# Attention probabilities turned by a transposing DMA instead of by TensorE

## The chip, the cores and the metric

The kernel runs on one core of one Trainium2 chip. The metric is the device time of one execution in microseconds (us). In the names of the profile PE is TensorE, PEld its weight loads, DVE is VectorE, ACT is ScalarE, POOL is GpSimd, SP is the engine whose queue issues most DMAs (SPq is that queue). `m_...` is an SBUF tensor, `bank` a PSUM bank.

## The reference

A residual stream x of 16 sequences of 64 tokens with 512 features (1024 tokens) passes eight blocks: four cross-attentions to a context of the same size, each followed by a feed-forward block. The change touches three of the attentions, which in the names are a0, a2 and a3. Each has 32 heads of size 128 and full fp32 accuracy is wanted. Layer 0 in short (a2 adds a position bias per head and a mask; a3 has 4 key/value heads and takes as keys the context and x itself, 128 for each sequence):

```
x = x + attention(layernorm(x), ctx)
q = rms(x @ Wq.T);  k = rms(ctx @ Wk.T);  v = ctx @ Wv.T     # 32 query heads, 8 key/value heads in a0
p = softmax(q @ k.T / sqrt(128))                             # per head: tokens x keys
out = (p @ v) @ Wo.T                                         # sums over 32 heads x 128
```

The product p @ v sums over keys. TensorE sums over partitions, so p, which is made with tokens on partitions, has to be turned: keys to partitions, tokens to columns.

## The kernel before

The blocks follow one another in time: set-up, a0 (about 55 to 656 us), its feed-forward f0, the cross-attention x1, f1 (to about 900), a2 (900 to 1670), f2, a3 (1855 to 2316), f3. All five engines run in parallel; only semaphores tie them.

Every fp32 product is done as three fp16 matmuls (`mm3`, L84, L85, L86): each operand is split into a high part (the value rounded to fp16) and a low part (the rest), and hi*hi, hi*lo and lo*hi are summed in PSUM. So whatever feeds a product is evicted twice, by ACT as the high part and by DVE as the low one (source minus high part).

An attention is 64 units: 8 groups of 4 heads, times 8 tiles of 128 tokens. The order of all work is one list of events, `events` (L125 to L194), from which each engine takes its own part and keeps its order. A slot of this list works on several units at once, in this order: scores of unit b; a projection tile (or several); the reciprocal of the row sums, `rinv`, of b; squares of a weight that has been loaded (`w_squares`); **turn** of b-1; **mix** of b-2, which is p @ v; **out** of b-3, which multiplies by Wo and adds to x; the split of the loaded weight (`w_convert`). Eight slots are a period; slots 0 to 3 and 4 to 7 serve the two halves of a group. `periods` writes period 0, a loop over the middle ones, and the last ones.

The steps of one unit and their lines:

- scores: PE into bank 2 or 3; DVE scales, adds mask or bias and takes the maximum (a0: L835, L852; a3: L823); ACT takes the exponential into `m_E` (L427, in a3 L423); DVE the reciprocal (L866); POOL multiplies `m_E` by it (L893), after which `m_E` holds probabilities in fp32, [128 tokens x 4 heads of 64 or 128 keys];
- turn: PE transposes `m_E` into bank 4 by fp32 matmuls with an identity, of 128 columns each (L611: two in a0, four in a2 and a3); ACT writes the high part from bank 4 to `m_PT` (L435) and DVE the low part (L870);
- mix: PE multiplies `m_PT` with the values into bank 5, ACT (L440) and DVE (L875) split that into `m_A`;
- out: PE multiplies `m_A` with `m_wo_t`, DVE adds the result to x (L881).

Weights come by DMAs that SP issues (`load`, L261), into the two halves of `m_raw`: 1 MB each, in a0 256 KB for k and v. SP first waits until the half is free (`w_lo`). ACT then squares the slab (L309), PE sums the squares over partitions (L481), and in a later slot ACT and DVE split it (L314, L680). In a2 SP also issues one 128 KB bias tile per unit (L285), for which it waits until the bias two units back has been used (`biased`). SP carries nothing else inside the attentions, so it stands at its next wait and issues each load as soon as the buffer is free. Loads stand in even slots of SP's program (a0 and a2: slots 0, 2, 4, 6; a3: slots 0, 2); squares stand in slots 0, 1, 4, 5 in a0, and in even slots elsewhere.

Semaphores count finished steps: `probs` is POOL's multiply, `turned` PE's transposes, `turned_hi` and `turned_lo` the two evictions, `mixed` PE's p @ v.

Of the kernel before, what the change touches and what calls it, by code (L numbers as in the profile page):

```python
# [7 lines left out]
FP16 = mybir.dt.float16  # L8
# [3 lines left out]
ALU = mybir.AluOpType  # L12
ACT = mybir.ActivationFunctionType
# [79 lines left out]
class Attention:  # L93
# [6 lines left out]
    def __init__(self, k, layer, dram, before, before_count):  # L100
# [10 lines left out]
        self.NP, self.NK = len(self.pre), len(self.kinds)  # L111
        names = ["raw0", "raw1", "w_ss", "w_tot", "w_scale", "w_fac", "w_hi", "w_lo", "misc", "misc_read",
                 "proj", "proj_hi", "proj_lo", "scores", "biased", "top", "exped", "rinv", "probs",
                 "turned", "turned_hi", "turned_lo", "mixed", "mixed_hi", "mixed_lo", "outp", "xadd",
                 "stat", "rstd", "xn", "xt", "xt_hi", "xt_lo", "dve", "pool"]
        names += {0: ["k_tot", "k_rs", "k_n", "k_nhi", "k_nlo", "q_tot", "q_rs"],
# [10 lines left out]
        totals |= dict.fromkeys(("scores", "top", "exped", "rinv", "probs", "turned", "turned_hi", "turned_lo",  # L127
                                 "mixed", "mixed_hi", "mixed_lo", "outp", "xadd"), UNITS)
        totals |= {"biased": 0 if layer == 3 else UNITS}
# [142 lines left out]
    def sp(self, sp):  # L272
# [13 lines left out]

        def emit(t, events):
            kinds = {7: 1, 8: 0}.get(t, self.NK) if isinstance(t, int) else self.NK
            for slot in range(8):
                if self.layer == 2 and (not isinstance(t, int) or 0 <= 8 * t + slot - 4 < UNITS):  # L290
                    bias(t, slot - 4)
                if slot % 2 == 0 and slot // 2 < kinds:
                    n, kind = slot // 2, self.kinds[slot // 2]
                    g = at(t, 1, 0 if kind == "o" else 1)
                    self.load(sp, kind, g, self.NP + self.NK * 0 + n + (self.NK * parity(t)),
                         at(t, self.NK, self.NP + n - 1))
                if isinstance(t, int) and t == 8 and slot == 1:
                    self.next.load_tail(sp)
# [47 lines left out]
    def act(self, act):  # L346
# [7 lines left out]
        def emit(t, events):  # L354
            for e in events:
# [59 lines left out]
                elif e[0] == "scores":  # L415
                    b = e[1]
                    act.wait_ge(*s["top"].by(at(t, 8, b + 1)))
                    act.wait_ge(*s["turned"].by(at(t, 8, b - 1)))
# [12 lines left out]
                elif e[0] == "turn":  # L431
                    b = e[1]
                    act.wait_ge(*s["turned"].by(at(t, 8, b + 1)))
                    act.wait_ge(*s["mixed"].by(at(t, 8, b - 1)))
                    act.activation(self.pt_dst(b, 0), bank[4][:, 0:self.keys * HG], ACT.Copy).then_inc(s["turned_hi"].sem, 1)  # L435
# [26 lines left out]
    def pt_dst(self, b, part):  # L462
        return self.k.PT[:, b % 2, part, 0:self.keys * HG]
# [31 lines left out]
    def pe(self, pe):  # L495
# [22 lines left out]
        def emit(t, events):  # L518
            par = parity(t)
            for e in events:  # L520
# [85 lines left out]
                elif e[0] == "turn":  # L606
                    b = e[1]
                    pe.wait_ge(*s["turned_lo"].by(at(t, 8, b)))
# [4 lines left out]
                elif e[0] == "mix":  # L613
# [3 lines left out]
                    pe.wait_ge(*s["turned_lo"].by(at(t, 8, b + 1)))  # L617
# [3 lines left out]
                    pt_ = k.PT[:, b % 2]  # L621
                    if self.layer == 0:
                        for b2 in range(2):
                            lhs = [k.V[:, i, hf, b2, pt * P:(pt + 1) * P] for i in range(2)]
                            ins = mm3(pe, out[:, b2 * HG * S:(b2 + 1) * HG * S], lhs, [pt_[:, i, 0:HG * S] for i in range(2)])
                    elif self.layer == 2:
                        for h in range(4):
                            cols = slice(h * P, (h + 1) * P)
                            ins = mm3(pe, out[:, cols], [k.V[:, i, hf, pt, cols] for i in range(2)],
                                      [pt_[:, i, cols] for i in range(2)])  # L630
                    else:
                        for b2 in range(2):
                            cols = slice(b2 * 256, (b2 + 1) * 256)
                            ins = mm3(pe, out[:, cols], [self.values3(t, b, i, b2) for i in range(2)],
                                      [pt_[:, i, cols] for i in range(2)])
# [101 lines left out]
    def dve(self, dve):  # L737
# [16 lines left out]
        def emit(t, events):  # L754
            par = parity(t)
            for e in events:
# [110 lines left out]
                elif e[0] == "turn":  # L867
                    b = e[1]
                    dve.wait_ge(*s["turned_hi"].by(at(t, 8, b + 1)))
                    dve.tensor_tensor(self.pt_dst(b, 1), bank[4][:, 0:self.keys * HG], self.pt_dst(b, 0),  # L870
                                      ALU.subtract).then_inc(s["turned_lo"].sem, 1)
# [716 lines left out]
class AdapterFFN(TailFFN):  # L1588
# [3 lines left out]
    def __init__(self, k, layer, att, dram):  # L1592
# [3 lines left out]
        super().__init__(k, f"f{layer}", ["iota", "hw", "ht", "ht_s", "out"], att, dram, n, regions)  # L1596
# [177 lines left out]
    def base(self, pe, t):  # L1774
# [4 lines left out]
        if t == 2:  # L1779
            pe.wait_ge(*a["turned_lo"].by(UNITS))  # L1780
# [236 lines left out]
class Kernel:  # L2017


    def __init__(self, nc, ctx):  # L2020
# [34 lines left out]
        self.PT, self.A = sb("PT", [P, 2, 2, 512], FP16), sb("A", [P, 2, 2, 512], FP16)  # L2055
        self.bias_in = sb("bias_in", [P, 2, 256])
# [226 lines left out]
```

## Time and profile before

| what | us |
|---|---|
| median of 3 runs | 2360.66 (2359.34 to 2363.18) |
| profiled execution, its own time | 2360.68 |
| span of that execution in the trace | 2358.9 |
| PE busy, share of the span | 2179.8 (92%) |
| DVE busy | 1335.0 (57%) |
| ACT busy | 1138.0 (48%) |
| POOL busy | 541.1 (23%) |
| PE's share of the chain that ended last | 65% |
| share of DVE, ACT, and of "issue" in that chain | 14%, 11%, 7% |

The chain is followed back from the last instruction of the program, each time to what released it. "issue" is time in which an engine waited for nothing that the profile shows. A busy share is a mean over stages with different limits; the stages have to be looked at one by one. The mean clock that TensorE was granted is 0.974 of full speed. The share of the DMA engines in use is around a tenth in most of the attentions.

### The profile page before, as it was taken

To read this page: it belongs to the slowest core of one execution; us is meant where nothing else is said; L and a number is where in the kernel's file an instruction comes from. 1 tells how busy PE (TensorE), PEld (TensorE's weight loads), DVE (VectorE), ACT (ScalarE), POOL (GpSimd) and SP (SyncE) were. 2 spreads that over 40 slices of the span, in tenths; PEclk is the share of its full clock that TensorE was granted. 3 is DMA by queue.
4 is the path that set the end of the run, shared out by engine and by line. 5 is a ranking of instruction groups with operands and counts; after the bars stand their busy time and mean duration, and the time that the engine had idled before them with its cause. 6 is when DMAs were issued, how large, how long until landed. Compare 5 with 4: busy or idle time off the path is not lost.

```text
span 2358.9 us, 40756 instructions
## 1 busy us (share of the span) xinstructions
PE 2179.8 (92%) x14284; PEld 1224.4 (52%) x14284; DVE 1335.0 (57%) x2695; ACT 1138.0 (48%) x2988; POOL 541.1 (23%) x936
## 2 busy tenths in 40 slices
PE   4889898988999889999999999998879899999998
PEld 2555555555554434555555555555434455555564
DVE  5566666666653455556565655655642455555554
ACT  4566565656412235545455554543322466556551
POOL 3332323233220222221222222112310122222221
PEclk8999999999979999999999999999979999999999
DMA  3110101100021011111112111101210101011000
GB/s 121 46 46 24 47 24 47 42 28 19 25 107 47 37 56 66 66 48 56 58 46 65 49 66 48 48 12 41 90 36 1 37 37 36 36 37 48 5 33 36
DMA packets 27365, 106.91 MB, mean 45 GB/s; under 512 B 4074, under 2 KB 12522, under 8 KB 17186
## 3 DMA queue, kind: packets, MB, share of 16 engines
q1 hardware_dynamic: 26722, 104.36, 12.8%
q8 instruction: 112, 1.84, 0.3%
q14 instruction: 83, 0.68, 0.1%
q10 hardware_dynamic: 448, 0.03, 0.0%
HBM read 102.29 MB, written 2.10 MB: 44 GB/s over the span
## 4 chain that ended last, share of the span: by engine, by line
PE 65%; DVE 14%; ACT 11%; issue 7%; POOL 1%; DMA 0%; ACTq 0%; DVEq 0%; POOLq 0%
PE bank L84 18%; PE bank L85 17%; PE bank L86 17%; PE bank L1786 3%; ACT m_E L427 2%; PE bank L1432 2%; PE bank L611 2%; DVE m_Sm L835 2%; DVE m_x L881 2%; ACT m_arena L309 2%; ACT m_arena L409 1%; DVE m_A L875 1%; PE bank L1332 1%; DVE m_arena L680 1%; DVE m_nmax L852 1%
## 5 line engine op out<-in xcount | busy, mean ns | idle before, releaser
L781 DVE TENSOR_TENSOR m_arena<-bank,m_arena 128x512 f16<-128x512 f32 x320 | 221.0, 691 | 506.7 <-ACT m_arena L409 504.9
L84 PE MATMUL bank<-m_input_parts,m_arena 128*128 128x512 f16 x1088 | 415.9, 382 | 8.4 <-DVE m_arena L781 2.3
L85 PE MATMUL bank<-m_input_parts,m_arena 128*128 128x512 f16 x1088 | 415.9, 382 | 0.0
L86 PE MATMUL bank<-m_input_parts,m_arena 128*128 128x512 f16 x1088 | 415.6, 382 | 0.0
L427 ACT ACTIVATE m_E<-m_Sm,m_nmax 128x64 f32<-128x64 f32 (+1 forms) x512 | 185.4, 363 | 421.1 <-DVE m_nmax L852 236.7
L893 POOL TENSOR_TENSOR m_E<-m_E,m_rinv 128x512 f32<-128x512 f32 (+1 forms) x192 | 177.6, 925 | 862.1 <-DVE m_rinv L866 862.1
L409 ACT ACTIVATE m_arena<-bank 128x512 f16<-128x512 f32 x320 | 189.7, 593 | 231.8 <-PE bank L86 231.3
L84 PE MATMUL bank<-m_wo_t,m_A 128*128 128x512 f16 x768 | 293.2, 382 | 0.0
L85 PE MATMUL bank<-m_wo_t,m_A 128*128 128x512 f16 x768 | 292.8, 381 | 0.0
L86 PE MATMUL bank<-m_wo_t,m_A 128*128 128x512 f16 x768 | 292.4, 381 | 0.0
L423 ACT ACTIVATE m_E<-bank,m_nmax,m_qk 128x128 f32<-128x128 f32 x256 | 113.8, 454 | 182.3 <-DVE m_nmax L823 182.3
L84 PE MATMUL bank<-m_arena,m_input_parts 128*128 128x128 f16 (+1 forms) x768 | 188.8, 276 | 5.5 <-DVE m_arena L786 4.7
L86 PE MATMUL bank<-m_arena,m_input_parts 128*128 128x128 f16 (+1 forms) x768 | 188.8, 276 | 0.0
L85 PE MATMUL bank<-m_arena,m_input_parts 128*128 128x128 f16 (+1 forms) x768 | 188.8, 276 | 0.0
L890 POOL TENSOR_TENSOR m_w_scale<-m_w_tot,m_consts 128x1 f32<-128x1 f32 x82 | 44.8, 546 | 584.4 <-DVE m_w_tot L674 551.7
L86 PEld LDWEIGHTS bank<-m_input_parts,m_arena 128*128 128x128 f16 x1088 | 107.2, 99 | 130.5 <-issue 3.7
L881 DVE SCALAR_TENSOR_TENSOR m_x<-bank,m_osc,m_x 128x512 f32<-128x512 f32 x192 | 143.1, 745 | 52.8 <-PE bank L86 52.5
L84 PEld LDWEIGHTS bank<-m_input_parts,m_arena 128*128 128x128 f16 x1088 | 107.1, 98 | 118.8 <-issue 5.7
L85 PEld LDWEIGHTS bank<-m_input_parts,m_arena 128*128 128x128 f16 x1088 | 107.0, 98 | 105.0 <-issue 3.7
L870 DVE TENSOR_TENSOR m_PT<-bank,m_PT 128x512 f16<-128x512 f32 (+1 forms) x192 | 112.2, 584 | 69.7 <-ACT m_PT L435 68.5
L611 PE MATMUL bank<-m_ident,m_E 128*128 128x128 f32 x640 | 104.1, 278 | 49.3 <-POOL m_E L893 49.2
L875 DVE TENSOR_TENSOR m_A<-bank,m_A 128x512 f16<-128x512 f32 x192 | 131.2, 683 | 0.2
(278 smaller groups left out, 4337.3 us busy)
## 6 DMA issues: line engine op xcount, KB each, us to landing
m_raw<-a_q SPq DMA_DIRECT2D x24, 1024.0 KB, 4.8
m_raw<-a_o SPq DMA_DIRECT2D x24, 1024.0 KB, 4.8
m_raw<-a_k SPq DMA_DIRECT2D x9, 1024.0 KB, 5.0
m_raw<-a_v SPq DMA_DIRECT2D x9, 1024.0 KB, 4.9
m_bias_in<-bias SPq DMA_DIRECT2D x64, 128.0 KB, 2.0
m_arena<-f_w SPq DMA_DIRECT2D x3, 1024.0 KB, 7.5
m_x<-x SPq DMA_DIRECT2D x2, 1024.0 KB, 6.9
m_arena<-ctx_t SPq DMA_DIRECT2D x4, 512.0 KB, 12.3
```

What stands on the lines that cost most here:

```text
L84: pe.matmul(out, lhs[0], rhs[0], start=first, stop=False)
L85: pe.matmul(out, lhs[0], rhs[1], start=False, stop=False)
L86: return pe.matmul(out, lhs[1], rhs[0], start=False, stop=last)
L409: act.activation(self.dest(name, part, 0), self.shaped(name, src), ACT.Copy).then_inc(s["proj_hi"].sem, 1)
L423: ins = act.activation(k.E[:, b % 2, cols], bank[2 + b % 2][:, cols], ACT.Exp, bias=k.nmax2[:, b % 2, h:h + 1], scale=qk, accum_out=k.rsum ...
L427: ins = act.activation(k.E[:, b % 2, cols], k.Sm[:, b % 2, cols], ACT.Exp, bias=k.nmax[:, b % 2, h:h + 1], accum_out=k.rsum[:, b % 2, h:h ...
L611: ins = pe.transpose(bank[4][:, j * P:(j + 1) * P], k.E[:, b % 2, j * P:(j + 1) * P], k.ident[:, :])
L781: ins = dve.tensor_tensor(self.dest(name, part, 1), self.shaped(name, bank[m % 2][:, :]), self.dest(name, part, 0), ALU.subtract)
L870: dve.tensor_tensor(self.pt_dst(b, 1), bank[4][:, 0:self.keys * HG], self.pt_dst(b, 0), ALU.subtract).then_inc(s["turned_lo"].sem, 1)
L875: dve.tensor_tensor(self.mix_dst(b, 1), self.mix_src(), self.mix_dst(b, 0), ALU.subtract).then_inc(s["mixed_lo"].sem, 1)
L881: dve.scalar_tensor_tensor(out=k.x[:, pair, :], in0=bank[6][:, :], scalar=k.osc[:, g:g + 1], in1=k.x[:, pair, :], op0=ALU.mult, op1=ALU.ad ...
L893: pool.tensor_tensor(out, a, b, op).then_inc(sem.sem, 1)
```

## The change

In a0, a2 and a3 (`self.moved` is true for all three) PE no longer transposes. In the step **turn**, ACT copies `m_E` from SBUF, as the high part in fp16, into a new SBUF tensor `m_split`; DVE subtracts it from `m_E` and writes the low part beside it; SP then issues one transposing DMA, which turns both parts of a unit into `m_PT`: [128 x 512] fp16 or 128 KB in a0, [128 x 1024] or 256 KB in a2 and a3. Mix on PE waits for the landing (`pt0`, `pt1`, one semaphore for each half of `m_PT`), not for DVE. SP waits, ahead of each transposing DMA, for the low part of the unit (`split_lo`) and for the mix of the unit two back, which frees `m_PT`. ACT waits, ahead of each high part, for the transposing DMA two units back, which frees `m_split`. ACT's exponential of a unit, which in before waited for PE's transposes of two units back, now waits for DVE's low part of it. In a0 the loads are in slots 0, 1, 4, 5 of SP's program instead of 0, 2, 4, 6. The event list, and with it the place of turn on ACT and DVE, is unchanged. Lines after the edits are 4 to 36 higher in the changed kernel.

```diff
@@ sp() @@
+        def turn(t, b):
+            n = 2 * HG * self.keys
+            sp.wait_ge(*s["split_lo"].by(at(t, 8, b + 1)))
+            sp.nop(nofuse=True)
+            sp.wait_ge(*s["mixed"].by(at(t, 8, b - 1)))
+            sp.nop(nofuse=True)
+            sp.dma_start_transpose(k.PT[:, b % 2].rearrange("p i n -> p (i n)")[:, 0:n].rearrange("p (h n) -> p h n", n=P),
+                                   k.split[:, b % 2].rearrange("p i n -> p (i n)")[:, 0:n])\
+                .then_inc((s["pt0"], s["pt1"])[b % 2].sem, 16)
...
                 if self.layer == 2 and (not isinstance(t, int) or 0 <= 8 * t + slot - 4 < UNITS):
                     bias(t, slot - 4)
-                if slot % 2 == 0 and slot // 2 < kinds:
-                    n, kind = slot // 2, self.kinds[slot // 2]
+                n = {0: 0, 1: 1, 4: 2, 5: 3}.get(slot, 4) if self.layer == 0 else 4 if slot % 2 else slot // 2
+                if n < kinds:
+                    kind = self.kinds[n]
                     g = at(t, 1, 0 if kind == "o" else 1)
                     self.load(sp, kind, g, self.NP + self.NK * 0 + n + (self.NK * parity(t)),
                          at(t, self.NK, self.NP + n - 1))
+                if self.moved and (not isinstance(t, int) or 0 <= 8 * t + slot - 5 < UNITS):
+                    turn(t, slot - 5)
@@ ScalarE @@
-                    act.wait_ge(*s["turned"].by(at(t, 8, b - 1)))
+                    act.wait_ge(*s["split_lo" if self.moved else "turned"].by(at(t, 8, b - 1)))
...
+                    if self.moved:
+                        act.wait_ge(*s["probs"].by(at(t, 8, b + 1)))
+                        act.wait_ge(*self.pt_here(t, b - 2))
+                        act.activation(self.split_dst(b, 0), k.E[:, b % 2, 0:self.keys * HG], ACT.Copy)\
+                            .then_inc(s["split_hi"].sem, 1)
+                        continue
@@ TensorE @@
-                elif e[0] == "turn":
+                elif e[0] == "turn" and not self.moved:
...
-                    pe.wait_ge(*s["turned_lo"].by(at(t, 8, b + 1)))
+                    pe.wait_ge(*(self.pt_here(t, b) if self.moved else s["split_lo"].by(at(t, 8, b + 1))))
@@ VectorE @@
+                    if self.moved:
+                        dve.tensor_tensor(self.split_dst(b, 1), k.E[:, b % 2, 0:self.keys * HG], self.split_dst(b, 0),
+                                          ALU.subtract).then_inc(s["split_lo"].sem, 1)
+                        continue
```

**SP in a0.** This is the end of the loop body of the middle periods in SP's program before. `m_raw<-a_o` is the load of a 1 MB slab of Wo; `w_lo` says that the buffer half is free.

```order
L261 DMA m_raw<-a_o 128x2048 [waits w_lo]
L252 REGISTER_ALU
L261 ISA [waits w_lo]
L261 DMA m_raw<-a_k 128x512
L252 REGISTER_ALU
L261 ISA [waits w_lo]
L261 DMA m_raw<-a_q 128x2048
L252 REGISTER_ALU
L261 DMA m_raw<-a_v 128x512 [waits w_lo]
L212 REGISTER_ALU
L212 COMPARE_AND_BRANCH
```

Four loads of a period stand in a row, with nothing between them but SP's wait for a free buffer half.

The same place in the program after, from the load of `a_o` on for four slots, L297 being the transposing DMA:

```order
L265 DMA m_raw<-a_o 128x2048 [waits w_lo]
L293 REGISTER_ALU
L297 DMA_TRANSPOSE m_PT<-m_split 128x4x128 [waits split_lo,mixed]
L256 REGISTER_ALU
L265 ISA [waits w_lo]
L265 DMA m_raw<-a_k 128x512
L293 REGISTER_ALU
L297 DMA_TRANSPOSE m_PT<-m_split 128x4x128 [waits split_lo,mixed]
L293 REGISTER_ALU
L297 DMA_TRANSPOSE m_PT<-m_split 128x4x128 [waits split_lo,mixed]
L293 REGISTER_ALU
L297 DMA_TRANSPOSE m_PT<-m_split 128x4x128 [waits split_lo,mixed]
```

Between a load and the next now stand transposing DMAs, each with its wait for DVE's low part of a unit. A load cannot be issued before the transposing DMA ahead of it in the list has been.

**SP in a3.** The start of the loop body in SP's program before:

```order
L212 ISA
L261 ISA [waits w_lo]
L261 DMA m_raw<-a_o 128x2048
L252 REGISTER_ALU
L261 ISA [waits w_lo]
L261 DMA m_raw<-a_q 128x2048
L252 REGISTER_ALU
L261 DMA m_raw<-a_o 128x2048 [waits w_lo]
```

Here too the loads follow on one another. The start of the loop body after:

```order
L265 ISA [waits w_lo]
L265 DMA m_raw<-a_o 128x2048
L293 ISA
L295 REGISTER_ALU [waits split_lo]
L297 DMA_TRANSPOSE m_PT<-m_split 128x8x128 [waits mixed]
L293 REGISTER_ALU
L295 REGISTER_ALU [waits split_lo]
L297 DMA_TRANSPOSE m_PT<-m_split 128x8x128 [waits mixed]
L256 REGISTER_ALU
L265 ISA [waits w_lo]
L265 DMA m_raw<-a_q 128x2048
```

The load of `a_q`, that followed directly on that of `a_o`, now stands behind the transposing DMAs of two slots. In a2 each slot also has its bias DMA, which stands ahead of the load and the transposing DMA of the same slot.

**PE in a3.** The end of a projection tile, turn and the start of mix in PE's program before:

```order
L85 MATMUL bank<-m_input_parts,m_arena 128x512
L86 MATMUL bank<-m_input_parts,m_arena 128x512
L609 REGISTER_ALU [waits turned_lo]
L611 MATMUL bank<-m_ident,m_E 128x128 [waits probs]
L611 MATMUL bank<-m_ident,m_E 128x128 x3
L84 ISA [waits turned_lo,mixed_lo]
L84 MATMUL bank<-m_PT,m_arena 128x256
L85 MATMUL bank<-m_PT,m_arena 128x256
L86 ISA
L86 MATMUL bank<-m_PT,m_arena 128x256
```

Turn stands between the tile and mix. The same place after:

```order
L85 MATMUL bank<-m_input_parts,m_arena 128x512
L86 MATMUL bank<-m_input_parts,m_arena 128x512
L648 REGISTER_ALU [waits mixed_lo]
L84 ISA [waits pt0]
L84 MATMUL bank<-m_PT,m_arena 128x256
L85 MATMUL bank<-m_PT,m_arena 128x256
L86 ISA
L86 MATMUL bank<-m_PT,m_arena 128x256
```

The four transposes of L611 are gone with their wait for POOL; mix starts right behind the projection tile and waits for the landing.

## Rows read from the trace of the kernel before

**Rows 1.** Busy by stretch: a0, a2, a3, one period of a3; columns: stretch, length, engines.
```profile
80.00:560.00 480.00, 428.84 (x3963) 268.04 (x3961) 307.10 (x719) 285.29 (x888) 148.95 (x251) 0.98 0.11 37
...
900.00:1620.00 720.00, 717.28 (x4514) 384.00 (x4512) 422.71 (x768) 360.42 (x860) 147.85 (x262) 1.00 0.15 50
...
1855.00:2270.00 415.00, 407.26 (x2701) 237.17 (x2700) 238.89 (x436) 246.65 (x693) 86.79 (x149) 1.00 0.09 31
...
2045.90:2102.60 56.70, 56.02 (x372) 32.64 (x370) 33.08 (x61) 34.29 (x96) 12.26 (x22) 1.00 0.11 37
```

**Rows 2.** Waits of ACT and PE, 80 to 560 us; columns: total us, times, longest.
```profile
ACT m_E L427 <- DVE m_nmax L852: 194.5, 52, 5.5
...
PE bank L611 <- POOL m_E L893: 32.0, 13, 2.6
```

**Rows 3.** Waits of PE, 900 to 1620 us: its only one.
```profile
PE bank L84 <- DVE m_arena L781: 2.7, 2, 1.9
```

**Rows 4.** Chain that ended last, a2; columns: start us, us, what.
```profile
1287.74 0.44 PE bank L611 x4
```

**Rows 5.** Waits of DVE on PE and of PE, 1945 to 2190 us.
```profile
DVE m_x L881 <- PE bank L86: 2.3, 7, 0.4
...
PE bank L481 <- ACT m_arena L309: 3.5, 5, 0.8
```

**Rows 6.** Timeline: low part, then squares of the next slot's load; a0, a3.
```profile
330.48 0.42 DVE L870 TENSOR_TENSOR m_PT<-bank,m_PT 128x256 f16<-128x256 f32 x1
...
336.19 1.90 ACT L309 ACTIVATE m_wo_t<-m_raw 128x2048 bf16<-128x2048 f32 x1
...
2102.95 0.66 DVE L870 TENSOR_TENSOR m_PT<-bank,m_PT 128x512 f16<-128x512 f32 x1
...
2108.69 1.92 ACT L309 ACTIVATE m_wo_t<-m_raw 128x2048 bf16<-128x2048 f32 x1
```

**Rows 7.** Timeline: low part, then its mix; a0, a2, a3, last unit.
```profile
310.71 0.39 DVE L870 TENSOR_TENSOR m_PT<-bank,m_PT 128x256 f16<-128x256 f32 x1
...
313.71 0.28 PE L84 MATMUL bank<-m_PT,m_arena 128*128 128x256 f16 x1
...
1292.22 0.69 DVE L870 TENSOR_TENSOR m_PT<-bank,m_PT 128x512 f16<-128x512 f32 x1 [1.39 <-ACT m_PT L435]
...
1302.77 0.22 PE L84 MATMUL bank<-m_PT,m_arena 128*128 128x128 f16 x1
...
2085.27 0.66 DVE L870 TENSOR_TENSOR m_PT<-bank,m_PT 128x512 f16<-128x512 f32 x1
...
2087.30 0.27 PE L84 MATMUL bank<-m_PT,m_arena 128*128 128x256 f16 x1
...
2303.62 0.68 DVE L870 TENSOR_TENSOR m_PT<-bank,m_PT 128x512 f16<-128x512 f32 x1
...
2304.96 0.28 PE L84 MATMUL bank<-m_PT,m_arena 128*128 128x256 f16 x1 [0.29 <-DVE m_A L875]
```

**Rows 8.** Page, group of the transposes: count, busy us, mean ns, idle before.
```profile
L611 PE MATMUL bank<-m_ident,m_E 128*128 128x128 f32 x640 | 104.1, 278 | 49.3 <-POOL m_E L893 49.2
```

**Rows 9.** SP's time for the issue of a copy: ns min/median/max.
```profile
L261 SPq DMA_DIRECT2D m_raw<-a_o x24: 328/333/423, 43.1 to 2178.4; - x24
```

**Rows 10.** Page, DMA issues: KB each, median us to landing.
```profile
m_raw<-a_o SPq DMA_DIRECT2D x24, 1024.0 KB, 4.8
...
m_bias_in<-bias SPq DMA_DIRECT2D x64, 128.0 KB, 2.0
```

**Rows 11.** DVE's L680, two inputs in SBUF, by itself: ns min/median/max.
```profile
L680 DVE SCALAR_TENSOR_TENSOR m_wo_t<-m_raw,m_w_scale,m_wo_t x25: 2341/2344/2352, 60.5 to 2232.8; 128x2048 f16<-128x2048 f32 x25
```

**Rows 12.** Timeline: POOL's multiply beside a low part (330.48), and beside L680.
```profile
330.53 0.61 POOL L893 TENSOR_TENSOR m_E<-m_E,m_rinv 128x256 f32<-128x256 f32 x1 [2.78 <-DVE m_rinv L866]
...
1907.93 1.04 POOL L893 TENSOR_TENSOR m_E<-m_E,m_rinv 128x512 f32<-128x512 f32 x1
1908.34 2.78 DVE L680 SCALAR_TENSOR_TENSOR m_arena<-m_raw,m_w_scale,m_arena 128x2048 f16<-128x2048 f32 x1 [0.26 <-ACT m_arena L314]
```

More of the change, by code:

```diff
@@ L126, in __init__ @@
         totals |= dict.fromkeys(("xn", "xt", "xt_hi", "xt_lo"), TILES)
-        totals |= dict.fromkeys(("scores", "top", "exped", "rinv", "probs", "turned", "turned_hi", "turned_lo",
+        totals |= dict.fromkeys(("scores", "top", "exped", "rinv", "probs", "split_hi", "split_lo",
                                  "mixed", "mixed_hi", "mixed_lo", "outp", "xadd"), UNITS)
+        totals |= {"turned": 0 if self.moved else UNITS}
+        totals |= dict.fromkeys(("pt0", "pt1"), 16 * (UNITS // 2) if self.moved else 0)
         totals |= {"biased": 0 if layer == 3 else UNITS}
@@ L432, in emit @@
                     b = e[1]
+                    if self.moved:
[4 more added lines that the diff above has]
+                        continue
                     act.wait_ge(*s["turned"].by(at(t, 8, b + 1)))
                     act.wait_ge(*s["mixed"].by(at(t, 8, b - 1)))
-                    act.activation(self.pt_dst(b, 0), bank[4][:, 0:self.keys * HG], ACT.Copy).then_inc(s["turned_hi"].sem, 1)
+                    act.activation(self.pt_dst(b, 0), bank[4][:, 0:self.keys * HG], ACT.Copy).then_inc(s["split_hi"].sem, 1)
                 elif e[0] == "mix":
@@ L462, in pt_dst, with split_dst, pt_here @@
     def pt_dst(self, b, part):
-        return self.k.PT[:, b % 2, part, 0:self.keys * HG]
+        n = self.keys * HG
+        return self.k.PT[:, b % 2].rearrange("p i n -> p (i n)")[:, part * n:part * n + n]
+    def split_dst(self, b, part):
+        n = self.keys * HG
+        return self.k.split[:, b % 2].rearrange("p i n -> p (i n)")[:, part * n:part * n + n]
+    def pt_here(self, t, b):
+        return (self.s["pt0"], self.s["pt1"])[b % 2].by(at(t, 64, 16 * (b // 2 + 1)))
     def mix_src(self):
@@ L620, in emit @@
                     out = bank[5]
-                    pt_ = k.PT[:, b % 2]
+                    pt_ = [self.pt_dst(b, i) for i in range(2)]
                     if self.layer == 0:
@@ L624, in emit @@
                             lhs = [k.V[:, i, hf, b2, pt * P:(pt + 1) * P] for i in range(2)]
-                            ins = mm3(pe, out[:, b2 * HG * S:(b2 + 1) * HG * S], lhs, [pt_[:, i, 0:HG * S] for i in range(2)])
+                            ins = mm3(pe, out[:, b2 * HG * S:(b2 + 1) * HG * S], lhs, pt_)
                     elif self.layer == 2:
@@ L629, in emit @@
                             ins = mm3(pe, out[:, cols], [k.V[:, i, hf, pt, cols] for i in range(2)],
-                                      [pt_[:, i, cols] for i in range(2)])
+                                      [pt_[i][:, cols] for i in range(2)])
                     else:
@@ L634, in emit @@
                             ins = mm3(pe, out[:, cols], [self.values3(t, b, i, b2) for i in range(2)],
-                                      [pt_[:, i, cols] for i in range(2)])
+                                      [pt_[i][:, cols] for i in range(2)])
                     ins.then_inc(s["mixed"].sem, 1)
```

15 lines of the change are left out of this document (9 added, 6 removed).

## The prediction

> **What bounds the kernel now.** I read the busy time by stage first, then the waits of each engine in a stage, then the chain, then single slots in the timeline. The stage table shows that the three attentions differ [rows 1]. In a2 PE is busy 717.28 of 720 us, and its waits add up to 2.7 us [rows 3]: PE sets the end, and a transposition on PE costs its full time, 0.44 us for four [rows 4]. In a0 PE is busy 428.84 of 480 us, DVE 307.10, ACT 285.29 [rows 1], so none is full. There ACT's one wait is for DVE, 194.5 us, and PE waits 32.0 us for POOL [rows 2]: ACT and DVE hand one unit's work to and fro, and PE has room. In a3 PE is busy 56.02 of a period of 56.70 us [rows 1], but DVE waits only 2.3 us for PE in 245 us, 7 times [rows 5]: PE and the pair of ACT and DVE have nearly the same length.
>
> **The change, part by part.** Against the profiled run, 2360.68 us; the median is 2360.66, so no conversion is needed.
>
> *Transposes off PE.* 640 go, 104.1 us of busy time [rows 8]; in the chain four cost 0.44 us, since they overlap in the pipeline [rows 4], so all are worth 70 us where PE is the bound. In a2 all but the last seven slots are: 57 x 0.44 = -25 us. In a3 DVE's wait for PE, 2.3 us in 4.3 periods [rows 5], is what can be taken from the pair: 0.53 a period, -4 over 7, and -3 in the seven tail slots with 0.44 each, where PE is nearly alone: -7. In a0 the bounds are 0 and 64 x 0.22 = -14, and a further -32 if PE's wait for POOL's multiply counted [rows 2]. It does not set the pace, since ACT waits for DVE and not for PE; I take -2, near the end of 0.
>
> *Two splits from SBUF instead of PSUM.* The same number of instructions of the same size on ACT and DVE. The low parts take 0.42 us in a0 and 0.66 in a3 [rows 6]; a tenth more or less of these in the 64 slots of a0 and of a3 would be +-7 us. I take 0. POOL's multiply no longer has to end before a transpose in the same slot on PE, but before ACT's copy of the same unit one slot later: nothing waits.
>
> *192 transposing DMAs on SP.* Before has none, so two unknowns: D, from the end of DVE's low part to the landing, and h, the time for which SP cannot issue what is queued behind. With h goes q, by which the transposition's data delay a load behind it. For D the nearest rows are 2.0 us for a copy of 128 KB and 4.8 for 1 MB [rows 10], with 128 KB and 256 KB to turn; turning is extra work and a copy's landing is the least, so I take 2.4 in a0 and 3.0 in a2 and a3. For h+q the ends are 0.33 us, a copy's issue [rows 9], and 4.8, if SP stands until landing. I take 1.5, which is between the copy's issue and its landing of 2.0; it is my least certain number.
>
> *Who waits for D.* Mix of a unit starts long after its low part: 2.61 us in the tightest slot of a0, 9.86 in a2, 1.37 in a3 [rows 7] (start less start and duration of the low part). In a0 2.4 fits. In a2 D is hidden, unless it were over 9. In a3 mix is later by 3.0 - 1.37 = 1.6 us; PE needs 56.0 - 8 x 0.44 = 52.5 of 56.7 us in a period now and can run behind by that. At worst both places a period where DVE waits for PE pay 1.6 - 0.44 each, 14 x 1.2 = +16; at best nothing. I take +2. The last unit of each attention has no other work to hide it: low part to mix was 0.66 us [rows 7], and this becomes D: 2 x 2.34 + 1.74 = +6.
>
> *Loads behind the transposing DMA.* This is the step that decides. SP issues the load of a slot only after the transposing DMA of the slot before, and this only after DVE's low part. Behind SP's wait stand the load, in a2 the next bias too, and ACT's squares wait for the load; ACT is half of the pair that bounds a0. In a0 a squares instruction on a 1 MB slab begins 336.19 - 330.90 = 5.29 us after the low part of the slot before [rows 6], and the load needs h+q and 4.8 us [rows 10]. Over is h+q - 0.49 = 1.0 us; o and q in seven periods and one more o are 15 such loads: +15. The 256 KB loads are smaller and have the time. In a3 the same gap is 2108.69 - 2103.61 = 5.08, less 0.44 as PE hands over earlier: h+q + 4.8 - 4.64 = 1.66 us, for the eight loads of Wo, +13. The loads of q there have squares two slots after o's and I take them as hidden. In a2 the slot is 12 us long and holds PE only; a late load or bias first uses up the pair's slack of several us: 0. If that cover were gone, each us would cost up to 57.
>
> *Sum.* a0 -2 + 15 = +13; a2 -25; a3 -7 + 2 + 13 = +8; the last units +6. Together +3: 2363.5 us. Each us of h+q moves it by 23.
>
> **The rivals.**
>
> *A. The transposing DMA is as cheap as a copy.* h+q = 0.33 and D = 2.0, the copy's rows. Then the 15 loads of a0 are in time, a3's eight pay 0.49 each: a0 -2, a2 -25, a3 -7 + 4, the last units +4: -26, 2335 us. For it: DMA engines are idle nine tenths of the time (share 0.11 to 0.15) [rows 1]. [...]
> [...]
>
> *B. SP stands until the transposition has landed.* h+q = D = 3.0: a0 -2 + 15 x 2.51 = +36, a2 -25, a3 -7 + 2 + 8 x 3.16 = +20, last units +6: +37, 2398 us. With 4.8 for all three: a0 +63, a3 +33 + 16, last units +12: +99, 2460. It decides from h+q = 1.6 on. [...] Against: a copy of 1 MB needs only 333 ns there [rows 9].
> [...]
>
> *C. A lock between DVE and POOL.* The low part now has two inputs in SBUF, as L680 has. L680 takes 2.34 us by itself [rows 11] but 2.78 when POOL's multiply had begun 0.41 us before [rows 12]. DVE's reciprocal frees POOL's multiply and is followed by the low part: at 330.48 DVE was first by 0.05 us [rows 6, 12]. If POOL came first, DVE would wait up to 0.6 us in a0 and 1.0 in a3. The timeline has the two side by side, on the chain, in about 70 slots of a0 and a3 (330.48 is the first kind of it, 4 heads of 64): 70 x 0.7 = +50 on top, 2413 us. Against: DVE is the earlier one in almost all.
> [...]
>
> *D. All of PE's time comes back.* 70 us and part of the 49.3 us that PE waited [rows 8]: some 2280. Against: PE has no place on the handing over between ACT and DVE in a0.
>
> **How the numbers follow.** My forecast, with h+q from 0.8 to 2.5, has .38, A .24, B .26, C .08, D .04. The measurement can tell 0.2%, 4.7 us. The forecast lies within that, but its own range is 2345 to 2387, since 0.2 us of h+q already crosses it: of .38, .06 is faster, .16 the same, .16 slower. Faster: .06 + .24 + .04 = .34; same .16; slower .16 + .26 + .08 = .50. The range of 8 in 10 reaches from A's time to above C's and into B's: 2334 to 2430.
>
> **What would show it.** The profile after has rows for the transposing DMA on SP: its time there is h, issue to landing is D's part. My steps are right if a2's slots shrink by 0.44 us each, if ACT waits for `m_raw` ahead of L309 in a0 15 times by about 1 us and in a3 8 times by 1.7, and PE waits for `m_PT` ahead of mix only at the three ends. A is right if these waits on `m_raw` are missing; B if SP's row is as long as the landing and the waits are over 2.5 us; C if the low part's mean grows by half. I am wrong as a whole if a2 does not get faster, which would mean that the bias or the loads come late there, or if D is beyond 5 us, so that every mix of a0 and a3 waits.

## The result: 2438 us, slower by 3.3%

| | median us | runs | ratio to before, 95% interval |
|---|---|---|---|
| before | 2361.92 | 2359.34 to 2364.53 | |
| changed kernel | 2438.12 | 2433.88 to 2440.76 | 1.0328 [1.0312, 1.0343] |
| forecast | 2363.5 | range 2334 to 2430 | |

The profiled executions took 2360.68 and 2433.88 us (spans 2358.9 and 2432.0), so the traces account for 73.1 us of the 76.2 between the medians. I split this by the starts of the 192 mixes on PE. "Body" is from the first mix of an attention to that of unit 56, "end" from there to the last unit's.

| us against before | body | last eight units | sum |
|---|---|---|---|
| a0 | +15.8 | +19.4 | +35.2 |
| a2 | -20.0 | +23.1 | +3.1 |
| a3 | +20.0 | +20.5 | +40.5 |
| other blocks | | | -5.7 |

The stage table of the changed kernel; columns as in rows 1. It answers to the first two of them, to a3 and to one period of a3.

```profile
80.00:560.00 480.00, 413.55 (x3774) 251.87 (x3773) 297.56 (x693) 281.96 (x863) 145.96 (x245) 0.97 0.17 48
900.00:1620.00 720.00, 713.15 (x4348) 364.06 (x4347) 423.63 (x771) 367.25 (x862) 182.60 (x271) 1.00 0.28 72
1905.00:2320.00 415.00, 370.76 (x2364) 200.50 (x2362) 229.35 (x416) 237.88 (x655) 97.00 (x146) 1.00 0.28 68
2045.78:2105.60 59.82, 53.16 (x340) 28.80 (x339) 33.20 (x62) 34.54 (x95) 14.02 (x23) 1.00 0.28 70
```

a2 is as full of PE as before [rows 1], and its slots fell by 0.44 us each, 12.14 to 11.70. In a3 PE fell from 407 to 371 us busy in 415: over a period it is no longer the bound, and a period is 59.8 us where it was 56.7. From mix to mix, the plain slots of a3 fell by the same 0.44 us (6.94 to 6.50), but three slots of a period rose, in the median from 7.0 to 9.4, from 7.8 to 9.7 and from 7.2 to 8.3 us. The other five are plain.

SP's own time for the transposing DMA (ns, minimum, median, maximum), and its time to landing; then, from the page, the landing of the copies and transpositions. They answer to [rows 9, 10].

```profile
L297 SPq DMA_TRANSPOSE m_PT<-m_split x192: 1189/1232/2472, 86.6 to 2374.9; - x192
...
DMA to landing us min/median/max: 2.4/3.0/4.8
```
```profile
m_raw<-a_o SPq DMA_DIRECT2D x24, 1024.0 KB, 4.9
...
m_bias_in<-bias SPq DMA_DIRECT2D x64, 128.0 KB, 2.2
m_PT<-m_split SPq DMA_TRANSPOSE x192, 3.0
```

So h is 1.2 us and the landing 2.4 us for 128 KB and 3.0 for 256 KB. To the landing come 0.13 us from the low part's end to SP's start and 0.14 from the landing to PE's: low part to mix is at least 2.65 us in a0 and 3.3 in a3.

**The body.** ACT's waits in a0 (80 to 560 us) and in a3 (1900 to 2320 us) of the changed kernel; the last line is a3's; columns: total us, times, longest.

```profile
ACT m_arena L326 <- DMA m_raw<-a_q: 6.8, 6, 1.5
ACT m_wo_t L326 <- DMA m_raw<-a_o: 5.0, 6, 1.3
...
ACT m_wo_t L326 <- DMA m_raw<-a_o: 10.7, 7, 1.9
```

ACT waits for the loads ahead of its squares as forecast: 11.8 us in 12 loads of a0, 0.98 each where 1.0 was forecast, and 1.5 in a3 where it was 1.66. Neither wait was there before.

**The ends.** Here is most of the loss, 63.0 of 73.1 us, and the prediction had 6. SP's queue and the router's matmuls of the block that follows a0, in the kernel before:

```profile
623.25 0.34 SPq L1124 DMA_DIRECT2D m_arena<-f_gate  x1
...
623.64 0.43 SPq L1124 DMA_DIRECT2D m_arena<-f_b  x1
...
631.21 0.96 PE L1168 MATMUL bank<-m_arena 128*128 128x8 f32 x8
```

and in the changed one, where the line numbers are 35 higher:

```profile
650.84 0.61 POOL L928 TENSOR_TENSOR m_E<-m_E,m_rinv 128x256 f32<-128x256 f32 x1 [2.37 <-DVE m_rinv L897]
650.89 0.84 DVE L902 TENSOR_TENSOR m_split<-m_E,m_split 128x256 f16<-128x256 f32 x1
...
651.86 1.19 SPq L297 DMA_TRANSPOSE m_PT<-m_split  x1
653.16 0.52 SPq L1159 DMA_DIRECT2D m_arena<-f_gate  x1
653.73 0.42 SPq L1159 DMA_DIRECT2D m_arena<-f_b  x1
...
658.75 1.88 PE L1203 MATMUL bank<-m_arena 128*128 128x8 f32 x8 [9.82 <-DMA m_arena<-f_b]
```

The blocks that follow an attention load their weights through the same queue (`load_tail`, five or so DMAs). Before, SP had nothing ahead of them and issued `f_b` 7.6 us before PE's router matmuls. Now the transposition of unit 60 stands ahead, and with it the wait for that unit's low part; `f_b` is issued 5 us before the matmuls, and PE waits 9.8 us for it. The chain of the changed kernel goes through it:

```profile
653.16 0.52 SPq L1159
...
653.73 4.98 DMA m_arena<-f_b
...
658.75 1.88 PE bank L1203 x8
660.62 0.44 PE bank L84
661.07 0.43 PE bank L85
```

The matmuls behind the wait take 0.43 us where they took 0.22. The granted clock is 0.50 there, the lower of the two levels in this trace (1.00 and 0.50), and stays so until 663.9: PE works 5.15 us at that level, which leaves some 2.6 us behind. In a2 the same wait is 14.4 us (for `f_bt`), in a3 11.0 (for `f_bm`): 35.2 us in the three.

The other part of the ends is the landing. PE's waits from 640 to 690 us of the changed kernel:

```profile
PE bank L84 <- DMA m_PT<-m_split: 10.2, 4, 3.1
PE bank L1203 <- DMA m_arena<-f_b: 9.8, 1, 9.8
```

Not one unit waits for its transposition at the end of an attention, but three to five (13.3 us in 3 waits in a2, 11.3 in 5 in a3): in the last period there are no projection tiles, and each slot is a chain of exponential, split, transposition, mix.

The lower clock costs more in the ends than behind these three waits. The three ends of the changed kernel, columns as in rows 1:

```profile
627.30:688.20 60.90, 40.83 (x325) 26.46 (x323) 34.93 (x86) 20.07 (x82) 17.56 (x20) 0.83 0.15 38
1615.90:1697.50 81.60, 51.14 (x329) 32.49 (x328) 39.93 (x79) 21.18 (x67) 19.07 (x20) 0.77 0.23 54
2316.00:2378.10 62.10, 39.80 (x252) 25.27 (x250) 32.36 (x62) 21.79 (x67) 15.70 (x16) 0.84 0.26 60
```

Before, the granted clock was 1.00, 0.94 and 1.00 in them. PE's work at the lower level rose from 6.8 to 36.3 us. Half of such work is lost, an estimate from the matmuls' 0.43 against 0.22 us, so the clock is some 15 of the 63 us. PE's idle time in the ends rose from 16.3 to 72.9 us.

### The profile page after: what moved, and what is told of

Its sections match the earlier page's. It is cut to its first block, busy times and chain, and to the rows that moved or that the text cites. A ratio compares the mean times of both kernels' runs of the same rounds, so it can differ in the third digit from the quotient of the medians.

```text
span 2432.0 us, 40109 instructions
## 1 busy us (share of the span) xinstructions
PE 2133.5 (88%) x13644; PEld 1158.0 (48%) x13644; DVE 1343.1 (55%) x2695; ACT 1145.5 (47%) x2988; POOL 595.5 (24%) x936
## 2 busy tenths in 40 slices
DMA packets 197347, 148.82 MB, mean 61 GB/s; under 512 B 174059, under 2 KB 182507, under 8 KB 187171
## 3 DMA queue, kind: packets, MB, share of 16 engines
q1 hardware_dynamic: 196706, 146.33, 21.8%
## 4 chain that ended last, share of the span: by engine, by line
PE 51%; DVE 15%; ACT 14%; issue 11%; DMA 6%; POOL 1%; SPq 1%; ACTq 0%; DVEq 0%; POOLq 0%
PE bank L84 13%; PE bank L86 13%; PE bank L85 13%; ACT m_E L444 2%; PE bank L1821 2%; PE bank L1467 2%; DMA m_raw<-a_o 2%; ACT m_E L440 2%; DMA m_PT<-m_split 2%; ACT m_arena L426 2%; DVE m_x L916 2%; DVE m_split L902 1%; DVE m_Sm L866 1%; PE bank L1367 1%; DVE m_arena L711 1%
## 5 line engine op out<-in xcount | busy, mean ns | idle before, releaser
L928 POOL TENSOR_TENSOR m_E<-m_E,m_rinv 128x512 f32<-128x512 f32 (+1 forms) x192 | 206.4, 1075 | 700.5 <-DVE m_rinv L897 700.5
L84 PE MATMUL bank<-m_wo_t,m_A 128*128 128x512 f16 x768 | 299.3, 390 | 0.0
L85 PE MATMUL bank<-m_wo_t,m_A 128*128 128x512 f16 x768 | 298.4, 389 | 0.0
L86 PE MATMUL bank<-m_wo_t,m_A 128*128 128x512 f16 x768 | 297.3, 387 | 0.0
L84 PE MATMUL bank<-m_PT,m_arena 128*128 128x256 f16 (+1 forms) x512 | 118.9, 251 | 80.5 <-DMA m_PT<-m_split 78.1
L902 DVE TENSOR_TENSOR m_split<-m_E,m_split 128x512 f16<-128x512 f32 (+1 forms) x192 | 119.4, 622 | 97.4 <-ACT m_split L453 96.3
```

The costliest lines, as they stand in the source:

```text
L84: pe.matmul(out, lhs[0], rhs[0], start=first, stop=False)
L85: pe.matmul(out, lhs[0], rhs[1], start=False, stop=False)
L86: return pe.matmul(out, lhs[1], rhs[0], start=False, stop=last)
L902: dve.tensor_tensor(self.split_dst(b, 1), k.E[:, b % 2, 0:self.keys * HG], self.split_dst(b, 0), ALU.subtract).then_inc(s["split_lo"].sem, 1)
L928: pool.tensor_tensor(out, a, b, op).then_inc(sem.sem, 1)
```

## Experiments

All ratios are to the kernel before on the same chip. The table gives the same split as above, in us against before.

| run | median us | ratio, 95% interval | a0 body, end | a2 body, end | a3 body, end |
|---|---|---|---|---|---|
| changed kernel | 2438.12 | 1.0328 [1.0312, 1.0343] | +15.8 +19.4 | -20.0 +23.1 | +20.0 +20.5 |
| e1_tail | 2406.37 | 1.0190 [1.0173, 1.0207] | +16.0 +10.4 | -20.2 +9.1 | +21.3 +8.3 |
| e2_queue | 2400.25 | 1.0155 [1.0138, 1.0172] | +3.2 +11.6 | +0.2 +15.5 | +2.2 +12.1 |
| e3_loads | 2410.71 | 1.0200 [1.0179, 1.0221] | +1.9 +19.6 | -22.8 +22.4 | +8.6 +20.7 |
| e4_both | 2376.30 | 1.0064 [1.0047, 1.0081] | +2.0 +6.6 | -22.8 +8.2 | +8.7 +10.2 |
| e5_only2 | 2344.41 | 0.9927 [0.9911, 0.9944] | -0.2 0.0 | -22.5 +8.9 | 0.0 0.0 |
| e6_only0 | 2369.27 | 1.0037 [1.0023, 1.0051] | +3.8 +12.1 | +1.1 +1.5 | +2.3 0.0 |
| e7_only3 | 2383.77 | 1.0095 [1.0079, 1.0112] | +0.4 +0.2 | +0.8 +1.5 | +9.6 +9.9 |
| e9_half | 2373.96 | 1.0059 [1.0042, 1.0076] | +0.8 0.0 | +0.9 +1.5 | +4.4 +8.7 |
| e8_best | 2339.03 | 0.9907 [0.9891, 0.9924] | +0.3 0.0 | -21.8 +1.0 | +0.1 0.0 |
| e10_squares | 2384.34 | 1.0098 [1.0076, 1.0120] | 0.0 0.0 | +0.9 +1.5 | +7.7 +11.4 |
| e11_before_sq | 2362.43 | 1.0007 [0.9997, 1.0018] | +0.2 0.0 | +0.2 0.0 | +1.0 0.0 |
| e12_two | 2347.65 | 0.9942 [0.9920, 0.9963] | +2.0 0.0 | -20.7 +0.8 | +7.1 -0.5 |

Bodies of attentions in which a run left the transposes on PE repeat to 2.3 us in this split, which is then its error. The time between the attentions moves by up to 5.8 us. The split belongs to the one profiled execution of a run, and this is not always near the median: that of e4_both is 7.8 us under it, that of e6_only0 5.0 above.

### e1_tail: the next block's loads earlier in the queue

```diff
+                if isinstance(t, int) and t == 8 and slot == 0:
+                    self.next.load_tail(sp)
                 if self.moved and (not isinstance(t, int) or 0 <= 8 * t + slot - 5 < UNITS):
                     turn(t, slot - 5)
-                if isinstance(t, int) and t == 8 and slot == 1:
-                    self.next.load_tail(sp)
```

> The changed kernel, with one edit: SP issues the loads of the feed-forward block that follows an attention ahead of the transposing DMA of unit 59 instead of behind that of unit 60. Theory T (the loads of the next block stand behind the transposing DMAs in SP's queue): PE's waits ahead of the router's matmuls (L1203), 9.8, 14.4 and 11.0 us in the changed kernel, go, and with them some 2 us each for matmuls at half clock behind them: 2438 - 41 = 2397 us, at most 2405. Theory H (the time is lost in the bodies of the attentions, by SP's 1.2 us for each transposition and by the landing): less than 3 us change, 2435 to 2438.

2406.37 us, 32 less. The bodies did not move. In the timeline of this run SP issues `f_b` ahead of unit 59's transposition, and PE's router matmuls have no wait:

```profile
639.15 1.19 SPq L297 DMA_TRANSPOSE m_PT<-m_split  x1
...
641.02 0.42 SPq L1159 DMA_DIRECT2D m_arena<-f_b  x1
...
645.59 7.48 SPq L297 DMA_TRANSPOSE m_PT<-m_split  x2
...
651.06 1.29 PE L1203 MATMUL bank<-m_arena 128*128 128x8 f32 x6
```

Theory T holds in its mechanism; it had expected 41 us, and the time came out 1 us above its limit of 2405. The profiled executions are 30.2 us apart. In them the three ends gave back 35.2 us, which is what the three waits were. The clock gave back less than the 2 us for each wait: PE's work at the lower level in the ends fell only from 36.3 to 29.4 us, as PE goes on waiting for its transpositions there (35.8 us, 34.8 in the changed kernel). The other 5 us are longer times in a3's body, between a2 and a3, and behind a3; no run shows why.

### e2_queue: the order of the queue without a transposition

```diff
@@ the kernel before, sp(); and loads in the slots of the changed kernel @@
+                if not isinstance(t, int) or 0 <= 8 * t + slot - 5 < UNITS:
+                    b = slot - 5
+                    sp.wait_ge(*s["turned_lo"].by(at(t, 8, b + 1)))
+                    sp.nop(nofuse=True)
+                    sp.wait_ge(*s["mixed"].by(at(t, 8, b - 1)))
+                    sp.nop(nofuse=True)
```

> The kernel before, with PE's transposes, in which SP only gets the waits of the changed kernel at the same places (DVE's low part of a unit, the mix two units back) and its slots of loads; no transposing DMA. It tells the order of the queue from the transposition's own time. Theory T: the next block's loads come behind the low part of unit 60, f_b lands at about 641 against a need at 631 in a0, the same in a2 and a3: three waits of about 10 us and 2 us each of half clock, 2362 + 36 = 2398 us; in the bodies the loads are just in time (5.2 against 5.3 us), 0 to 5 us more. Theory H: without a transposition there is nothing to lose, 2362 to 2366.

2400.25 us: 38 us slower than before with not one transposition moved. The kernel's PE waits from 600 to 660 us, from 2310 to 2345 and from 1630 to 1690 us show the three waits of theory T, 34 us together:

```profile
PE bank L1175 <- DMA m_arena<-f_b: 10.3, 1, 10.3
...
PE bank L1175 <- DMA m_arena<-f_bm: 11.1, 1, 11.1
...
PE bank L1175 <- DMA m_arena<-f_bt: 12.8, 1, 12.8
```

So half of a loss of 76 us comes from the order of one queue, without the price of a single transposition; most of it lies in the ends (39.2 us of the profiled execution's 43.9), as in the changed kernel.

### e3_loads and e4_both: weight loads one slot earlier

```diff
@@ in place of the choice of n for each slot @@
+                due = [(t, n) for n in range(1, kinds)
+                       if slot == ({1: 0, 2: 3, 3: 4}[n] if self.layer == 0 else 2 * n - 1)]
+                if t == 0 and slot == 0:
+                    due.insert(0, (t, 0))
+                if slot == 7 and t not in (7, 8):
+                    due.append((t + 1 if isinstance(t, int) else (t[0], t[1] + 1), 0))
+                for u, n in due:
```

> The changed kernel, in which each weight load stands one slot earlier in SP's queue, ahead of the transposing DMA that it followed; the loads of the next block stay where they are. Theory of the prediction (ACT's squares wait for the load): ACT's waits for m_raw, 11.8 us in 12 loads of a0 and 6.5 in 4 of a3, go: 15 x 1.0 + 8 x 1.6 = 28 us less, 2410. Rival L (the landing of the transposition takes the place of the load at once, as PE waits for m_PT in a3 already): a0 gains 15, a3 under 4, 2420. Rival: squares were not on the path, under 5 us change.

2410.71 us, 27 less: the expected number. ACT has no wait for `m_raw` left in a0 or a3. The bodies fell by 13.9 us in a0 and by 11.4 in a3, against 15 and 13 in the prediction. Rival L is wrong for a3: PE's other waits did not take the place of this one.

e4_both has this edit and that of e1_tail.

> Both edits of the two runs before it in the changed kernel: next block's loads early and weight loads one slot early. If they add up: 2438 - 41 - 28 = 2369 us; by rival L 2379. What then is left against the kernel before (2362) is the landing of the transpositions in a3's slots and in the last units, less the 25 us that a2 gains.

2376.30 us, 62 less than the changed kernel against 59 of the two single runs (32 and 27): they add up. It is 7 above the 2369 expected, which is what e1_tail had lacked already. What is left over the kernel before is 14 us, with a2's body at its full gain.

### e5_only2, e6_only0, e7_only3: one attention at a time

Each has both repairs and `self.moved = layer in (2,)`, `(0,)` or `(3,)`.

> Only a2 turns by transposing DMA; a0 and a3 turn on PE as in the kernel before; both repairs of SP's queue (weight loads one slot early, next block's loads ahead of unit 59's transposition). In the run with all three attentions a2's body was 22.8 us shorter than before and its last eight slots 8.2 us longer. If the layers are independent: 2362.4 - 14.6 = 2348 us. If what a0 or a3 did to later blocks matters (the time from a0's last mix to a2's first was 5.8 us shorter), up to 5 us off.

> Only a0 turns by transposing DMA, with both repairs of SP's queue. In the run with all three, a0's body was 2 us longer than before, its last eight slots 6.6 us longer, and the way from there to a2 5.8 us shorter: 2362 + 9 = 2371 us if that last number was chance, 2365 if it comes with a0's change.

> Only a3 turns by transposing DMA, with both repairs of SP's queue. Theory D (PE waits for the landing, 17.2 us in 13 waits of 230 us): body +8.7, last slots +10.2: 2362.4 + 19 = 2381 us. It is the base for the run with half the data.

2344.41, 2369.27 and 2383.77 us. They add: -16, +8 and +23 us make +15, and e4_both was +14. So a2 gains from the change, a0 loses a little, and a3 loses most. a0's end was +12.1 in e6_only0 where it was +6.6 in e4_both. This is the clock: PE was idle for 10.9 and 9.9 us there, but the granted clock was 0.84 against 0.93, and PE's work at the lower level was 16.3 us against 6.8. The way from there to a2 was 4.9 us shorter again, as in all runs in which a0 was turned by DMA, but also by 4.0 in e7_only3, where it was not, and by 0.0 in e10_squares, where it was not either. That number moves by itself.

### e9_half: half the data in a3

```diff
-            n = 2 * HG * self.keys
+            n = HG * self.keys
...
-                    pt_ = [self.pt_dst(b, i) for i in range(2)]
+                    pt_ = [self.pt_dst(b, 0 if self.moved else i) for i in range(2)]
```

> As the run with a3 alone, but only the high parts of the probabilities are turned; the low parts are left out, and mix takes the high part twice in their place, so that PE, ACT and DVE do the same instructions. The transposition is 128 KB instead of 256 KB. Theory D: low part to mix falls from 3.3 us to the 2.65 of a0's 128 KB, at some 3.2 waits a period and in the last four units: 7 x 3.2 x 0.65 + 4 x 0.65 = 17 us less, 2381 - 17 = 2364. Theory P (a3 loses by DVE's and POOL's shared access to SBUF and by the order of waits, not by the landing): under 4 us less, 2377 to 2381.

2373.96 us, 9.8 less than e7_only3. The transposing DMA's rows of e7_only3 (256 KB) and of this run (128 KB), each with its landing:

```profile
L297 SPq DMA_TRANSPOSE m_PT<-m_split x64: 1232/1233/2109, 1865.5 to 2321.4; - x64
...
DMA to landing us min/median/max: 3.0/3.1/4.3
```
```profile
L297 SPq DMA_TRANSPOSE m_PT<-m_split x64: 1189/1191/2163, 1864.5 to 2314.1; - x64
...
DMA to landing us min/median/max: 2.4/2.5/3.5
```

PE's waits for the landing, 1900 to 2130 us, e7_only3 and then e9_half:

```profile
PE bank L84 <- DMA m_PT<-m_split: 17.4, 12, 1.8
```
```profile
PE bank L84 <- DMA m_PT<-m_split: 12.3, 11, 1.7
```

The landing is part of a3's cost: 0.6 us of it took 5.2 us off the body, 0.74 a period. Of the 9.8 us only 6.4 lie in a3 (1.2 in its end); the rest is in blocks that the edit does not touch. Theory D had 17 us, so it is too high by more than double, and Theory P, with under 4, is too low. From mix to mix the gain is in one slot of a period, 7.4 to 6.8 us. The two longest stay at 9.7 and 8.3, where before had 7.8 and 7.2, and half of the body's loss stays with them. And h did not follow the size: 1.23 us for 256 KB, 1.19 for 128.

### e10_squares and its control e11_before_sq: squares behind turn in a3

```diff
-            if squared is not None:
+            if squared is not None and self.layer != 3:
                 out.append(("w_squares", squared))
             if ok(b - 1):
                 out.append(("turn", b - 1))
+            if squared is not None and self.layer == 3:
+                out.append(("w_squares", squared))
```

> The kernel with a3 alone turned by DMA (2383.8 us) with one edit: in a3's event list the squares of a loaded weight (1.9 us on ACT) stand behind turn instead of ahead of it. In the trace of that kernel the slots that carry squares are 9.8 and 8.3 us where they were 8.0 and 7.0, and the chain there runs: exponential, squares, high part, low part, transposition 3.1 us, mix. Theory D+S (the landing adds to squares that stand ahead of the high part): both slots get shorter, 2.6 us a period, 2384 - 18 = 2366 us. Rival (squares behind turn only delay ACT's next item, the split of the mix or the tile's high part, which then holds PE): under 5 us less, over 2379.

> Control for the run beside it: the kernel before, with PE's transposes, with a3's squares behind turn. There the low part is followed by its mix at once when PE is there; slots with squares were longer than the plain ones by 1.0 and 0.9 us. Theory D+S: it gains little, 0 to 6 us, 2355 to 2361. If it gains as much as the other one, the order of the squares is a fault of its own that has nothing to do with the transposition's landing.

2384.34 us against 2383.77 of e7_only3, and 2362.43 for the control against 2361.43: no change in either. My theory D+S fell. Waits of e10_squares from 1945 to 2190 us:

```profile
DVE m_A L917 <- ACT m_A L470: 13.9, 9, 1.5
...
PE bank L519 <- ACT m_arena L333: 8.9, 4, 2.3
...
PE bank L84 <- DMA m_PT<-m_split: 5.8, 6, 1.4
```

The edit did what it was to do: PE's wait for the landing is 5.8 us, in the same stretch of e7_only3 18.1. The squares then hold the next items, the split of the mix (13.9 us on DVE) and PE's sum of squares (8.9 us, 4.3 in e7_only3). But together PE's waits fell by 7.7 us, and the time did not. The trace shows where it went. Behind PE's wait for the squares the granted clock falls to its lower level for 3.4 us, once in each period of e10_squares; e7_only3 has no such stretch from 1875 to 2294 us. The same 4.4 us of a period in e10_squares, with the wait ahead of them and the mix behind, and then in e7_only3:

```profile
2080.61 0.18 PE L519 MATMUL bank<-m_w_ss,m_ones_b 128*128 128x1 bf16 x1 [2.31 <-ACT m_arena L333]
...
2084.97 0.27 PE L84 MATMUL bank<-m_PT,m_arena 128*128 128x256 f16 x1
...
2080.60:2085.00 4.40, 4.39 (x14) 1.73 (x15) 2.23 (x5) 2.12 (x9) 0.00 (x0) 0.61 0.31 60
```
```profile
2076.00:2080.40 4.40, 2.84 (x13) 1.16 (x13) 2.84 (x6) 2.00 (x9) 0.14 (x1) 1.00 0.31 60
```

In e10_squares the twelve matmuls of the tile took 4.3 us in place of 2.6, and mix followed them without a wait; its transposition had landed 2.2 us earlier. In e7_only3 PE ended the tile early and waited 1.7 us for the landing. So the landing no longer holds this slot after the edit, and the clock took back about 1.7 us a period, an estimate from these rows. Over a3's body PE's idle time fell from 34.8 to 24.3 us, and its busy time rose from 369.8 to 378.3. What the place of the squares is worth at the full clock is not shown.

### e8_best and e12_two: what the experiments point to

```diff
+    def by_dma(self, t):
+        return self.moved and t != 8
...
+        return self.s["turned"].by(b + 6 if self.moved else at(t, 8, b + 1))
```

e8_best uses the transposing DMA in a2 alone, for units 0 to 58; the last five units take the old way over PE, bank 4 and `m_PT`. e12_two does so in a2 and a3, with a3's squares behind turn.

> Only a2 turns by transposing DMA, and only units 0 to 58; the five units of its last period, which have no other work beside them, turn on PE. Weight loads one slot early; next block's loads at the old place, where no transposition is left beside them. a2's body -22.8, last slots as before: 2362.4 - 23 = 2339 to 2341 us. If the bias or something else of a2 is late it stays above 2345.

> The fastest kernel so far (a2 alone by DMA, its last five units on PE, 2339 us) with a3 by DMA too, again but for the last five units, and with a3's squares behind turn. If a3's body loses 10 us by the landing and the squares' place gives 18 back, and the last slots cost nothing: 2339 - 8 = 2331 us. If the landing keeps PE waiting in the plain slots too, 2339 to 2345.

e8_best: 2339.03 us, 0.9907 [0.9891, 0.9924] of before, as expected. It beats both kernels. Against e5_only2 a2's end fell from +8.9 to +1.0: the last units by DMA cost 7.9 us in one attention, landing and clock together, and 5.4 us between the medians. e12_two: 2347.65, 9 above, and 3 past the second branch of its expectation. a3's body stays at +7.1, but not because of waits in the plain slots, as that branch had it: these are 6.5 us, shorter than before. The slot with the squares is 10.8 us, and the granted clock falls in it once a period, as in e10_squares.

## Why the prediction was wrong

The forecast of 2363.5 and the range to 2430 missed 2438. (The rounded terms of its sum give +2, the unrounded ones +3.) Step by step:

- **Transposes off PE in a2, -25.** Right: 0.44 us a slot; the body gained 20.0 us in the changed kernel and 22.8 with early loads.
- **Two splits from SBUF, taken as 0.** Nearly right. ACT's high part rose from 522 to 555 ns in the mean and DVE's low part from 584 to 622, some 7 us of busy time each over 192 units.
- **h + q, taken as 1.5 with ends 0.33 and 4.8.** Right enough: 1.2 us on SP and a wait of 0.98 in a0, 1.5 in a3, where 1.0 and 1.66 stood. e3_loads took these waits away.
- **D, taken as 2.4 and 3.0.** Landing right; with SP's start and PE's it is 2.65 and 3.3.
- **D in a3's slots, +2.** Mis-sized. With the load waits gone a3's body is +8.7 instead of the -2 that this step (+2) and PE's transposes (-4) gave. PE was to wait for `m_PT` only at the three ends; in a3's body it waits 33.7 us in 20 waits. e9_half shows that 0.6 us of landing is worth 5 us there; the remainder is not settled.
- **"The last unit of each attention", +6.** Wrong in its count. Three to five units of each end wait for their transposition, 34.8 us of PE's waits in the three ends (10.2, 13.3 and 11.3 us); in a2, e8_best took 7.9 us off the end.
- **The clock, for which the sum had no term.** PE's work at the lower level in the ends costs an estimated 15 us more than before. e1_tail removed the three long waits and kept most of this.
- **The step that failed: "Loads behind the transposing DMA".** It counted the weight loads and biases of the same attention and put nothing for the loads of the next block, which stand in the same queue, behind the transposition of unit 60. SP's program of the changed kernel had them there, with three transpositions behind (L1159 and L1161 are `load_tail`):

```
L265 DMA m_raw<-a_o 128x2048 [waits w_lo]
L297 DMA_TRANSPOSE m_PT<-m_split 128x4x128 [waits split_lo,mixed] x10
L1159 DMA m_arena<-f_gate 128x32 [waits misc_read,proj_lo]
L1159 DMA m_arena<-f_b 128x512
L1161 DMA m_arena<-f_w 128x2048
...
L297 DMA_TRANSPOSE m_PT<-m_split 128x4x128 [waits split_lo,mixed] x3
```

  The waits are 9.8, 14.4 and 11.0 us, e1_tail took back 32, and e2_queue showed 38 without any transposition. With their 35 us the same sum would have been 2399, within the range; the ends' other units, the clock and a3's body make up the rest.

The rivals: A is out, since h is 1.2. B, SP standing until the landing, is out as well: h is 1.2 us and the landing 3.0, though the time came out beyond B's 2398. Nor does h follow the size: half the data took 1.19 us in place of 1.23. The landing is near that of a copy: 3.0 us for 256 KB, where a copy of 256 KB (`m_raw<-a_v`) landed in 2.7. What C expected does occur, in the last units: at 650.84 POOL came first by 0.05 us and the low part took 0.84 us instead of 0.42. This happened to twelve low parts, four in each end (0.84 us in a0, 1.53 in a2, 1.33 in a3), and not to one in the bodies: not 70 slots, and 7.2 us of DVE's time in all. In the bodies it is POOL that got slower, its multiply from 1.04 to 1.28 us in a3's, and ACT's high part never waited for it. D is out: in a0, where PE has room, no gain was seen (its body +2.0 us in e4_both, +3.8 in e6_only0).

**What stays open.** In a3 PE is idle for 3.5 to 5 us a period and the body is still 7 to 10 us longer than before, once loads are early. 0.6 us of landing explains about half. Moving the squares moves a part of the wait and brings the lower clock, and the two can't be told apart here. I have not taken ACT's squares out or given `m_PT` a third buffer, which would tell whether the loop of ACT and DVE or the two buffers set it.

## What to carry to other kernels

Before a DMA that waits for late work is put into a queue, list everything that is issued behind it in program order, past the end of the loop and into the next block, and find for each what needs it; the longest waits here belonged to another block. The transfer that replaced matmuls gained where TensorE was the bound and other units' work covered its landing (a2's body, -20.0 us), and cost its landing where the pipeline ran dry (34.8 us of PE's waits in the three ends). TensorE's granted clock was lower there too (0.77 to 0.84 in the three ends here), so a run that removes or moves waits has to be read with its granted clock beside it. So apply it by stage and leave the old way at the ends: of three attentions one gained, and with its last units on TensorE it gave 0.9%.

## What I had not expected of the hardware

- A transposing DMA from SBUF to SBUF held SP for 1.19 us at 128 KB and 1.23 us at 256 KB, where most copies, of up to 1 MB, held it for 0.33 to 0.53. Between these two sizes the cost in the queue hardly moves.
- It is made of small pieces: the packets of the whole run rose from 27,365 to 197,347, and those under 512 B from 4,074 to 174,059, and still the 1 MB loads landed in 4.9 us instead of 4.8. By this median the contention q was 0.1 us for them.
- After the wait of 9.8 us on PE the next matmuls of 512 columns ran at 0.43 us in place of 0.22 (granted clock 0.50), and PE worked 5.15 us at this level, so that wait cost about 2.6 us more than its length.
- Which of DVE and POOL was slowed, when a low part and POOL's multiply began side by side in a0, turned on which began first: where POOL did by 0.05 us (at 650.84), the low part took 0.84 us in place of 0.42 and the multiply 0.61; where DVE did by 0.17 (at 638.62), the low part took 0.39 us and the multiply 0.70.
